# One core, a fused graph layer: offsets in slots of 16 words, norm statistics a tile ahead, one edge load and one one-hot per tile

## Chip, cores and metric

One Trainium2 chip, one core. The metric is the device time in microseconds (us) of one execution of the program. The kernel works in fp32; TensorE multiplies either fp32 or pairs of fp32r halves (a "hi" part and what is left of it, "lo").

## The reference

12,500 nodes with 128 features, 200,000 edges with 48 features, `dst` sorted. What is computed, cut to its core:

```python
h = jnp.maximum(_layernorm(x, axis=-1), 0.0)
agg_edge = jax.ops.segment_sum(edge_attr_48, dst, num_segments=12500)     # 12500 x 48
collected = jnp.concatenate([h, agg_edge], axis=1)                        # 12500 x 176
u = jax.nn.silu(collected @ W1 + b1)                                      # 256 wide
u = jax.nn.silu(u @ W2 + b2)                                              # 256 wide
out = x + h + (u @ W3 + b3)                                               # 12500 x 128
```

The only irregular part is the segment sum: the rows of `edge_attr` are added up by their destination.

## The kernel before

The nodes are cut into `NT` = 28 tiles of 448 nodes (the last one 404), the sorted edges into 391 groups of 512, 14 groups to a tile (`GPT`), seven to a half (`HALF`). A group lies on 128 partitions with four edges each. Its edges hit a window of at most 42 neighbouring nodes, so its sum is a matrix product: a one-hot matrix (edge against node of the window) made by VectorE's `onehot_of`, times the edges' features. `sum_tile` does this for 14 groups into the PSUM bank `stage`; ScalarE copies it to `staged` (`stage_sums`); `place_batch` then adds each group's 42 columns at the right place of the tile's bank `agg_ps`, by a matrix product with the identity whose output address is a register. Those registers are the group's **offsets**: 14 integers of `offset_row`, an SBUF tensor with one word per group, which `offsets_of` loads into registers of TensorE's sequencer. Batch `b` takes groups 14b-3 to 14b+10 (`EARLY` = 3); batch 0 takes 11 (words 0 to 10), the last one 16.

Every engine runs its own program; semaphores tie them together. The order of work is written out by hand in the `step` functions, one step per tile: steps 1 to 3 unrolled, 4 to 21 in a loop that does two steps a turn, 22 to 29 unrolled (`pipeline`). In step i

- TensorE does layer 1 of tile i-1, `offsets_of(i+1)`, `sum_tile(i+1)`, layer 3 of tile i-2, the transposes of tile i, `place_batch(i+1)`, layer 2 of tile i-1, in this order;
- VectorE does `relu_lo(i-1)`, `carry_over(i-1)`, the norm statistics of tile i (`load_stats`, bn_stats over x), `agg_lo(i-1)`, `aggregate_stats(i)`, the first one-hot half of tile i+2, `shift_of_norm(i)`, the lo parts of h1 and `add_x(i-1)`, the second one-hot half, `add_b3(i-1)`, and `finish(i-2)`, which makes the output tile;
- GpSimd does one power, (var+eps)^-0.5 (`rstd_of(i)`);
- ScalarE does the relu and hi parts, the SiLUs of layers 2 (tile i-2) and 1 (tile i-1), the normalised x (`normalize(i)`) and `stage_sums(i+1)`;
- SyncE issues all DMAs: first edge half of tile i+3, x of tile i+1, second edge half of tile i+3, store of tile i-2. Each waits in SyncE's queue until its buffer is free: the edge halves for `s_summed` (a half summed in step i), x for `s_plain` (`add_x(i-1)` is done, the last reader of that x buffer), the store for `s_out` (`finish(i-2)`).

Edges, one-hots and x are double buffered by the tile's parity.

Of the kernel before, what the change touches and what calls it, by code (L numbers as in the profile page):

```python
# [25 lines left out]
ALU = mybir.AluOpType  # L26
# [7 lines left out]
def gnn_kernel(nc, x, dst, edge_attr, W1, b1, W2, b2, W3, b3, out):  # L34
# [3 lines left out]
    P = 128  # L38
# [26 lines left out]
    assert N * GROUP == NPG * E and E % PER == 0 and N % PER == 0  # L65
    PAIRS = GPT // 2
# [16 lines left out]
    with ExitStack() as ctx:  # L83
        def sb(name, shape, dt=F32):
            return ctx.enter_context(nc.sbuf_tensor(name, shape, dt))
# [38 lines left out]
        offset_row = sb("offset_row", [1, ROWS * P], I32)  # L124
# [88 lines left out]
        s_edges = [sem(f"edges_loaded{k}") for k in range(4)]  # L213
# [71 lines left out]
        def _(sp):  # L285
# [5 lines left out]
            def load_edges(i, parity, half):  # L291
                n, full = groups_of(i, half)
                slot = 2 * parity + half

                wait(sp, s_summed, 2 * (i - 2) + half + 1)
                e0 = (i * GPT + half * HALF) * GROUP
                sp.dma_start(raw[:, slot, 0:full].rearrange("p g j d -> p g (j d)"),  # L297
                             edge_attr[bass.ds(e0, full * GROUP), :].rearrange(
                                 "(g p j) d -> p g (j d)", p=P, j=PER)).then_inc(s_edges[slot], 16)
                if full < n:  # L300
                    sp.dma_start(raw[0:TAIL_P, slot, full].rearrange("p j d -> p (j d)"),
                                 edge_attr[E - TAIL_P * PER:E, :].rearrange(
                                     "(p j) d -> p (j d)", j=PER)).then_inc(s_edges[slot], 16)
# [42 lines left out]
            for t in (2, 3):  # L346
                for half in range(2):
                    load_edges(t, t % 2, half)
# [16 lines left out]
            def step(i, parity):  # L365
                if has(i, -3, NT):
                    load_edges(i + 3, 1 - parity, 0)
                if has(i, -1, NT):
                    load_x(i + 1, 1 - parity)
                if has(i, -3, NT):  # L370
                    load_edges(i + 3, 1 - parity, 1)
                if has(i, 2, NT):
                    store(i - 2, parity)
# [8 lines left out]
        def _(pool):  # L382
# [23 lines left out]
            def step(i, parity):  # L406
                if has(i, 0, NT):
                    rstd_of(i, parity)
# [3 lines left out]
            pool.iota(tile_i[:, :], pattern=[[1, TILE]], base=0, channel_multiplier=0).then_inc(s_pool_zero, 1)  # L412
            pipeline(pool, step)
# [115 lines left out]
        def _(dve):  # L529
# [106 lines left out]
            def make_onehot(i, parity, half):  # L636

                wait(dve, s_summed, 2 * (i - 2) + half + 1)
                onehot_of(i, parity, half).then_inc(s_onehot, 1)

# [12 lines left out]
            dve.tensor_copy(offset_row[:, 0:P], z3[0:1, 0, :]).then_inc(s_off0, 1)  # L653
# [21 lines left out]
            dve.tensor_copy(offset_row[:, P:], z3[0:1, 1:ROWS, :].rearrange("p q d -> p (q d)"))  # L675
# [3 lines left out]
            for half in range(2):  # L679
                make_onehot(2, 0, half)  # L680

            def general_path():
# [31 lines left out]
                dve.wait_ge(s_onehot, 6)  # L714
# [93 lines left out]
            def step(i, parity):  # L808
                if has(i, 1, NT):
                    relu_lo(i - 1)  # L810
                    carry_over(i - 1, 1 - parity)
                if has(i, 0, NT):
                    load_stats(i, parity)
                    dve.wait_ge(s_stats, i + 1)
                if has(i, 1, NT):
                    agg_lo(i - 1)
                if has(i, 0, NT):
                    aggregate_stats(i, parity)
                if has(i, -2, NT):
                    make_onehot(i + 2, parity, 0)  # L820
                if has(i, 0, NT):
                    shift_of_norm(i, parity)
# [4 lines left out]
                if has(i, -2, NT):  # L827
                    make_onehot(i + 2, parity, 1)
# [8 lines left out]
        def _(pe):  # L837
# [63 lines left out]
            def sum_tile(i, parity):  # L901
# [160 lines left out]
```

## Time and profile before

| | |
|---|---|
| median of 3 runs | 417.44 us (416.64 to 420.57) |
| the profiled execution: its own time, and its span | 418.25 us, 416.5 us |
| busy share of the span: TensorE matmuls, weight loads | 80%, 72% |
| VectorE, ScalarE, GpSimd | 64%, 51%, 15% |
| mean granted TensorE clock | 0.967 of full speed |
| DMA | 53.07 MB, mean 127 GB/s |

The span runs from the first to the last instruction; the 1.75 us beside it are start and end of the execution. A row of a timeline says when a run of instructions of one line started, how long it took, and in brackets how long its engine had been idle before it and which event ended that idleness; "issue" means that the profile shows nothing that the engine waited for. Rows of the sequencers (PEldq: TensorE's, SPq: SyncE's) are register, branch and DMA instructions and are not counted as busy.

### The profile page before, as it was taken

How to read it: one execution, taken by the hardware profiler on the slowest of the kernel's cores; microseconds unless marked ns; L12 is line 12 of the kernel's file. 1: busy time of each engine (PE TensorE's matmuls, PEld its weight loads, DVE VectorE, ACT ScalarE, POOL GpSimd, SP SyncE). 2: the span in 40 equal slices, each digit the busy share in tenths (PEclk: the TensorE clock that was granted, in tenths of full speed). 3: DMA queues.
4: the chain of work that ended last, by engine and by line, in shares of the span. 5: the costliest groups of instructions: out<-in, count | busy, mean ns of one | idle time of the engine just before them, and what ended most of it. 6: DMA issues, size and time to landing. Idle time of an engine off the chain costs nothing.

```text
span 416.5 us, 13441 instructions
## 1 busy us (share of the span) xinstructions
PE 331.1 (80%) x5150; PEld 300.3 (72%) x5151; DVE 267.1 (64%) x634; ACT 213.9 (51%) x406; POOL 60.8 (15%) x44
## 2 busy tenths in 40 slices
PE   6556777977797779877897779777977798778885
PEld 6445777966687668866787669666966787677875
DVE  7954558566766686668656766667566765785443
ACT  7643446346644564455544653456346644465372
POOL 2101011012211222022202220122012110110000
PEclk9967969999999999999999999999999999999999
DMA  7970524633664256533663356435632675340101
GB/s 215 290 216 2 155 58 124 178 105 84 169 176 132 82 138 176 160 89 104 176 171 91 94 172 176 107 82 164 176 106 77 171 179 147 101 121 24 44 22 43
DMA packets 79194, 53.07 MB, mean 127 GB/s; under 512 B 2912, under 2 KB 78778, under 8 KB 79168
## 3 DMA queue, kind: packets, MB, share of 16 engines
q1 hardware_dynamic: 79168, 52.70, 46.1%
q8 instruction: 19, 0.31, 0.3%
q14 instruction: 7, 0.06, 0.0%
HBM read 46.29 MB, written 6.40 MB: 127 GB/s over the span
## 4 chain that ended last, share of the span: by engine, by line
PE 40%; issue 21%; DMA 20%; DVE 13%; ACT 3%; SPq 2%; DVEq 0%; POOL 0%; ACTq 0%; POOLq 0%
DMA x_t<-in_x_dram 20%; PE stage L919 16%; PE z L997 6%; DVE onehot L632 6%; PE agg_ps L936 4%; DVE stats L606 3%; PE z L982 3%; PE z L986 2%; PE z L983 2%; SPq L297 2%; DVE meanvar L612 2%; PE tp L949 1%; PE z L965 1%; PE z L970 1%; PE z L971 1%
## 5 line engine op out<-in xcount | busy, mean ns | idle before, releaser
L919 PE MATMUL stage<-onehot,raw 128*48 128x42 f32 x3128 | 81.8, 221 | 61.7 <-issue 60.8
L919 PEld LDWEIGHTS stage<-onehot,raw 128*48 128x48 f32 x3128 | 78.7, 132 | 71.4 <-issue 71.3
L403 POOL TENSOR_TENSOR rstd<-vareps,minus_half 112x4 f32<-112x4 f32 (+1 forms) x28 | 57.6, 2059 | 334.9 <-DVE vareps L616 334.9
L632 DVE TENSOR_TENSOR onehot<-window,rel 128x1176 f32<-128x1176 f32 (+1 forms) x56 | 76.9, 1375 | 2.7 <-ACT rel L433 1.3
L805 DVE TENSOR_TENSOR out_t<-z,resid 112x512 f32<-112x512 f32 (+1 forms) x28 | 19.4, 691 | 71.3 <-PE z L997 71.3
L997 PE MATMUL z<-w,h 128*112 128x128 f32 (+1 forms) x448 | 56.2, 278 | 0.9 <-ACT h L491 0.8
L997 PEld LDWEIGHTS z<-w,h 128*112 128x112 f32 (+1 forms) x448 | 50.8, 177 | 2.7 <-issue 1.4
L441 ACT ACTIVATE staged<-stage 112x294 f32<-112x294 f32 x28 | 11.6, 416 | 68.4 <-PE stage L919 68.4
L936 PE MATMUL agg_ps<-staged,ident 112*48 112x42 f32 x782 | 42.5, 219 | 5.1 <-issue 5.1
L470 ACT ACTIVATE xn<-x_t,nmr,rstd 112x128 f32<-112x128 f32 (+1 forms) x112 | 45.9, 480 | 0.1
L936 PEld LDWEIGHTS agg_ps<-staged,ident 112*48 112x48 f32 x782 | 39.2, 129 | 9.2 <-issue 5.7
L491 ACT ACTIVATE h<-z,b2c 128x448 f32<-128x448 f32 (+1 forms) x56 | 35.0, 626 | 17.2 <-PE z L986 17.2
L982 PE MATMUL z<-h_hi,w_hi 128*128 128x448 f32 (+1 forms) x112 | 43.8, 391 | 0.0
L499 ACT ACTIVATE h<-z,b1c 128x448 f32<-128x448 f32 (+1 forms) x56 | 35.0, 624 | 15.9 <-PE z L971 15.9
L478 ACT ACTIVATE hT_hi<-tp 128x448 fp32r<-128x448 f32 (+1 forms) x28 | 15.2, 542 | 51.3 <-PE tp L949 51.2
L983 PE MATMUL z<-h_hi,w_lo 128*128 128x448 f32 (+1 forms) x112 | 40.8, 365 | 0.0
L779 DVE TENSOR_TENSOR h_lo<-h,h_hi 128x448 fp32r<-128x448 f32 (+1 forms) x56 | 34.7, 620 | 5.1 <-ACT h_hi L503 5.0
L484 ACT ACTIVATE agg_hilo<-agg 48x448 fp32r<-48x448 f32 (+1 forms) x28 | 16.1, 577 | 40.5 <-DVE agg L755 40.5
L606 DVE BATCH_NORM_STATS2 stats<-x_t 112x6 f32<-112x128 f32 (+1 forms) x112 | 24.4, 279 | 16.9 <-DMA x_t<-in_x_dram 16.8
L503 ACT ACTIVATE h_hi<-h 128x448 fp32r<-128x448 f32 (+1 forms) x56 | 32.2, 575 | 1.8
L986 PE MATMUL z<-h_lo,w_hi 128*128 128x448 f32 (+1 forms) x112 | 31.9, 365 | 0.0
L772 DVE SCALAR_TENSOR_TENSOR hT_lo<-tp,hT_hi 128x448 fp32r<-128x448 f32 (+1 forms) x28 | 17.4, 623 | 12.5 <-ACT hT_hi L478 12.5
(108 smaller groups left out, 415.9 us busy)
## 6 DMA issues: line engine op xcount, KB each, us to landing
raw<-in_edge_attr_dram SPq DMA_DIRECT2D x55, 672.0 KB, 6.2
x_t<-in_x_dram SPq DMA_DIRECT2D x27, 224.0 KB, 5.3
out_dram<-out_t SPq DMA_DIRECT2D x27, 224.0 KB, 4.6
dst_rows<-in_dst_dram SPq DMA_DIRECT2D x1, 512.0 KB
raw<-in_edge_attr_dram SPq DMA_DIRECT2D x1, 480.0 KB, 5.8
dst_rows<-in_dst_dram SPq DMA_DIRECT2D x1, 256.0 KB, 2.7
out_t<-in_L_gnn_W_dram SPq DMA_DIRECT2D x1, 256.0 KB, 8.2
x_t<-in_x_dram SPq DMA_DIRECT2D x1, 192.0 KB
```

Of the source, the lines that this page charges most:

```text
L403: pool.tensor_tensor(rstd[0:np_, parity], vareps[0:np_, :], minus_half[0:np_, :], ALU.pow).then_inc(s_rstd, 1)
L470: ln = act.activation(xn[0:np_, parity, q, :], x_t[0:np_, parity, q, :], ACT.Identity, bias=nmr[0:np_, parity, q:q + 1], scale=rstd[0:np_, ...
L491: act.activation(h2[:, m, 0:n], z[:, m, 0:n], ACT.Silu, bias=b2c[:, m:m + 1]).then_inc(s_h2, 1)
L499: act.activation(h1[:, m, 0:n], z[:, m, 0:n], ACT.Silu, bias=b1c[:, m:m + 1]).then_inc(s_h1, 1)
L606: st = dve.bn_stats(stats[0:np_, q, :], x_t[0:np_, parity, q, :])
L632: return dve.tensor_tensor(onehot[:, slot, 0:n * PER, :], window[:, :].unsqueeze(1).broadcast_to([P, n * PER, WINDOW]), cols.unsqueeze(2). ...
L919: mm = pe.matmul(stage[at:at + ED, pair * WINDOW:(pair + 1) * WINDOW], raw[0:rows, 2 * parity + half, k, j, :], onehot[0:rows, 2 * parity ...
L936: mm = pe.matmul(banks[0:ED, bass.ds(offset, WINDOW)], ident[0:ROW2 + ED, at:at + ED], staged[:, parity if k >= 0 else 1 - parity, group / ...
L982: pe.matmul(z[:, m, 0:n], w2_hi[:, k, cols], h1_hi[:, k, 0:n], start=(k == 0), stop=False)
L983: pe.matmul(z[:, m, 0:n], w2_lo[:, k, cols], h1_hi[:, k, 0:n], start=False, stop=False)
L986: mm = pe.matmul(z[:, m, 0:n], w2_hi[:, k, cols], h1_lo[:, k, 0:n], start=False, stop=(k == M - 1))
L997: mm = pe.matmul(z3[0:np_, q, :], h2[:, k, q * np_:(q + 1) * np_], w3[:, k, :], start=(k == 0), stop=(k == M - 1))
```

## The change

- `offset_row` gets a slot of 16 words per batch (`SLOT`), with group k of batch b (k from -3) at word 16b+k+3. VectorE fills it with three strided copies in place of one, twice. `offsets_of(b)` reads from word 16b (batch 0 from word 3). The number of words that are loaded stays 11, 14 and 16.
- The statistics, the power and the shift of the norm run one tile ahead, for tile i+1 in step i; tile 1's are made before the first step.
- VectorE's order in a step is new: `add_x`, `carry_over`, `relu_lo`, `agg_lo`, one-hots of tile i+2, `load_stats(i+1)`, `add_b3`, `aggregate_stats(i+1)`, both lo parts, `shift_of_norm(i+1)`, `finish`.
- SyncE's order is x, edges, store. From tile 2 on the edges of a tile are one DMA (waiting until the whole of the tile before in that buffer is summed) and its one-hots one instruction; TensorE waits once for each per tile.

```diff
+    SLOT = 16
-        offset_row = sb("offset_row", [1, ROWS * P], I32)
+        offset_row = sb("offset_row", [1, NT * SLOT], I32)
...
+            def load_tile(i, parity):
+                full = sum(groups_of(i, half)[1] for half in range(2))
+                slots = raw[:, 2 * parity:2 * parity + 2].rearrange("p s g j d -> p (s g) (j d)")
+
+                wait(sp, s_summed, 2 * (i - 2) + 2)
+                sp.dma_start(slots[:, 0:full], edge_attr[bass.ds(i * GPT * GROUP, full * GROUP), :].rearrange(
+                    "(g p j) d -> p g (j d)", p=P, j=PER)).then_inc(s_edges[parity], 16)
...
             def step(i, parity):
-                if has(i, -3, NT):
-                    load_edges(i + 3, 1 - parity, 0)
                 if has(i, -1, NT):
                     load_x(i + 1, 1 - parity)
                 if has(i, -3, NT):
-                    load_edges(i + 3, 1 - parity, 1)
+                    load_tile(i + 3, 1 - parity)
                 if has(i, 2, NT):
                     store(i - 2, parity)
...
             def step(i, parity):
-                if has(i, 0, NT):
-                    rstd_of(i, parity)
+                if has(i, -1, NT):
+                    rstd_of(i + 1, 1 - parity)
...
+            def make_onehots(i, parity):
+
+                n = sum(groups_of(i, half)[0] for half in range(2))
+                wait(dve, s_summed, 2 * (i - 2) + 2)
+                cols = rel[:, :, :].rearrange("p g j -> p (g j)")[:, bass.ds(i * GPT * PER, n * PER)]
+                slots = onehot[:, 2 * parity:2 * parity + 2].rearrange("p s e w -> p (s e) w")
+                dve.tensor_tensor(slots[:, 0:n * PER, :],
+                                  window[:, :].unsqueeze(1).broadcast_to([P, n * PER, WINDOW]),
+                                  cols.unsqueeze(2).broadcast_to([P, n * PER, WINDOW]),
+                                  ALU.is_equal).then_inc(s_onehot, 1)
...
-            dve.tensor_copy(offset_row[:, 0:P], z3[0:1, 0, :]).then_inc(s_off0, 1)
+            offsets_into(0, EARLY, GPT)
+            offsets_into(1, 0, GPT, FULL0 - 1)
+            offsets_into(FULL0, 0, REST0).then_inc(s_off0, 1)
...
-            dve.tensor_copy(offset_row[:, P:], z3[0:1, 1:ROWS, :].rearrange("p q d -> p (q d)"))
+            offsets_into(FULL0, REST0, GPT)
+            offsets_into(FULL0 + 1, 0, GPT, NT - 2 - FULL0)
+            offsets_into(NT - 1, 0, NG + EARLY - (NT - 1) * GPT)
...
-            for half in range(2):
-                make_onehot(2, 0, half)
+            load_stats(1, 1)
+            dve.wait_ge(s_stats, 2)
+            aggregate_stats(1, 1)
+            make_onehots(2, 0)
+            shift_of_norm(1, 1)
...
             def step(i, parity):
                 if has(i, 1, NT):
+                    add_x(i - 1, 1 - parity)
+                    carry_over(i - 1, 1 - parity)
                     relu_lo(i - 1)
-                    carry_over(i - 1, 1 - parity)
-                if has(i, 0, NT):
-                    load_stats(i, parity)
-                    dve.wait_ge(s_stats, i + 1)
+                    agg_lo(i - 1)
+                if has(i, -2, NT):
+                    make_onehots(i + 2, parity)
+                if has(i, -1, NT):
+                    load_stats(i + 1, 1 - parity)
+                    dve.wait_ge(s_stats, i + 2)
                 if has(i, 1, NT):
-                    agg_lo(i - 1)
...
+                    add_b3(i - 1, 1 - parity)
+                if has(i, -1, NT):
+                    aggregate_stats(i + 1, 1 - parity)
                 if has(i, 1, NT):
                     h1_lo_part(i - 1, 0)
-                    add_x(i - 1, 1 - parity)
                     h1_lo_part(i - 1, 1)
...
-                if has(i, 1, NT):
-                    add_b3(i - 1, 1 - parity)
+                if has(i, -1, NT):
+                    shift_of_norm(i + 1, 1 - parity)
                 if has(i, 2, NT):
                     finish(i - 2, parity)
...
-                    offset_row[0:1, bass.ds(b * GPT + first, last - first)], engines=[mybir.EngineType.PE],
+                    offset_row[0:1, bass.ds(b * SLOT + (first + EARLY), last - first)], engines=[mybir.EngineType.PE],
...
                         if k % HALF == 0:
-                            pe.wait_ge(s_edges[slot], 16 * slot_turn(i, parity) + (16 if full < n else 0))
-                            pe.wait_ge(s_onehot, 2 * i + k // HALF + 1)
+                            if isinstance(i, int) and i < 2:
+                                pe.wait_ge(s_edges01[slot], 16)
+                                pe.wait_ge(s_onehot, 2 * i + k // HALF + 1)
+                            elif k == 0:
+                                pe.wait_ge(s_edges[parity], 16 * (slot_turn(i, parity) - 1) + (16 if total < GPT else 0))
+                                pe.wait_ge(s_onehot, i + 3)
```

## Rows read from the trace of the kernel before

**Rows 1.** Windows of two tile periods: us; PE, PEld, DVE, ACT, POOL busy; PEclk; DMA

```profile
181.61:195.20 13.59, 11.15 (x182) 10.14 (x183) 9.33 (x22) 7.08 (x15) 2.11 (x1) 1.00 0.50 135
195.20:208.75 13.55, 11.09 (x183) 10.14 (x183) 9.50 (x23) 7.08 (x16) 2.24 (x1) 1.00 0.46 135
```

**Rows 2.** Timeline, TensorE in the period from 181.61 (start, us, engine, line)

```profile
178.78 0.36 PE L971 MATMUL z<-agg_hilo,w1e_lo 112*128 112x448 f32 x1
...
181.61 2.72 PE L919 MATMUL stage<-onehot,raw 128*48 128x42 f32 x112 [2.46 <-issue]
...
190.54 0.37 PE L965 MATMUL z<-hT_hi,w1x_hi 128*128 128x448 f32 x1
...
195.20 2.72 PE L919 MATMUL stage<-onehot,raw 128*48 128x42 f32 x112 [2.44 <-issue]
...
199.69 0.55 PE L949 MATMUL tp<-ident,xn 112*128 112x112 f32 x4
```

**Rows 3.** The waits view, TensorE's sums (us in total, times, longest)

```profile
PE stage L919 <- issue: 60.8, 26, 2.6
```

**Rows 4.** Line L892, the offsets' register load, in five windows: ns min/median/max

```profile
L892 PEldq TENSOR_LOAD <-offset_row x18: 3332/3336/3344, 83.0 to 315.2; - x18
...
L892 PEldq TENSOR_LOAD <-offset_row x1: 1520/1520/1520, 27.3 to 27.3; - x1
...
L892 PEldq TENSOR_LOAD <-offset_row x1: 3343/3343/3343, 28.9 to 28.9; - x1
...
L892 PEldq TENSOR_LOAD <-offset_row x1: 3336/3336/3336, 178.0 to 178.0; - x1
...
L892 PEldq TENSOR_LOAD <-offset_row x1: 3800/3800/3800, 382.4 to 382.4; - x1
```

**Rows 5.** Line L270 on TensorE's sequencer: the load of one word

```profile
L270 PEldq TENSOR_LOAD <-any_invalid x1: 319/319/319, 32.3 to 32.3; - x1
```

**Rows 6.** Timeline, the early stretch around tiles 1 to 4

```profile
51.02 0.87 DVE L606 BATCH_NORM_STATS2 stats<-x_t 112x6 f32<-112x128 f32 x4 [3.74 <-DMA x_t<-in_x_dram]
...
52.60 0.47 PE L970 MATMUL z<-agg_hilo,w1e_hi 112*128 112x448 f32 x1 [2.12 <-DVE agg_hilo L765]
...
56.13 4.71 PE L919 MATMUL stage<-onehot,raw 128*48 128x42 f32 x112 [1.83 <-issue]
```

**Rows 7.** Timeline, VectorE, ScalarE and GpSimd from 184.82 to 197.49

```profile
186.30 0.69 DVE L805 TENSOR_TENSOR out_t<-z,resid 112x512 f32<-112x512 f32 x1 [2.29 <-PE z L997]
...
187.99 0.61 DVE L755 TENSOR_TENSOR agg<-agg_ps,agg_carry 48x448 f32<-48x448 f32 x1
...
189.16 0.87 DVE L606 BATCH_NORM_STATS2 stats<-x_t 112x6 f32<-112x128 f32 x4 [0.43 <-DMA x_t<-in_x_dram]
...
190.06 0.62 DVE L765 TENSOR_TENSOR agg_hilo<-agg,agg_hilo 48x448 fp32r<-48x448 f32 x1
...
190.71 0.38 DVE L612 BATCH_NORM_AGGREGATE meanvar<-stats 112x2 f32<-112x6 f32 x4
...
191.38 1.38 DVE L632 TENSOR_TENSOR onehot<-window,rel 128x1176 f32<-128x1176 f32 x1
191.52 2.11 POOL L403 TENSOR_TENSOR rstd<-vareps,minus_half 112x4 f32<-112x4 f32 x1 [11.28 <-DVE vareps L616]
...
194.06 1.63 ACT L470 ACTIVATE xn<-x_t,nmr,rstd 112x128 f32<-112x128 f32 x4
194.37 0.68 DVE L786 SCALAR_TENSOR_TENSOR resid<-xn,x_t 112x512 f32<-112x512 f32 x1
...
196.80 0.69 DVE L796 TENSOR_TENSOR resid<-resid,b3r 112x512 f32<-112x512 f32 x1
```

**Rows 8.** The DMA view from 182 to 196: issues, KB each, us to landing

```profile
raw<-in_edge_attr_dram SPq DMA_DIRECT2D x2, 672.0 KB, 6.0
x_t<-in_x_dram SPq DMA_DIRECT2D x1, 224.0 KB, 5.1
```

**Rows 9.** x loads (L310) over the whole run: min/median/max to landing

```profile
DMA to landing us min/median/max: 2.7/5.3/7.5
```

More of the change, by code:

```diff
@@ L212, in gnn_kernel @@
         s_carry0_act = sem("carry_zeroed_by_act")
-        s_edges = [sem(f"edges_loaded{k}") for k in range(4)]
+        s_edges01 = [sem(f"edges_of_0_and_1_loaded{k}") for k in range(4)]
+        s_edges = [sem(f"edges_loaded{k}") for k in range(2)]
         s_onehot = sem("onehot_ready")
@@ L291, in load_edges @@
             def load_edges(i, parity, half):
-                n, full = groups_of(i, half)
-                slot = 2 * parity + half
-                wait(sp, s_summed, 2 * (i - 2) + half + 1)
                 e0 = (i * GPT + half * HALF) * GROUP
[L297 to L303, printed above, removed]
+                sp.dma_start(raw[:, 2 * parity + half].rearrange("p g j d -> p g (j d)"),
+                             edge_attr[bass.ds(e0, HALF * GROUP), :].rearrange(
+                                 "(g p j) d -> p g (j d)", p=P, j=PER)).then_inc(s_edges01[2 * parity + half], 16)
+            def load_tile(i, parity):
[4 more added lines that the diff above has]
+                    "(g p j) d -> p g (j d)", p=P, j=PER)).then_inc(s_edges[parity], 16)
+                if full < GPT:
+                    sp.dma_start(slots[0:TAIL_P, full], edge_attr[E - TAIL_P * PER:E, :].rearrange(
+                        "(p j) d -> p (j d)", j=PER)).then_inc(s_edges[parity], 16)
             def load_x(t, parity):
@@ L346, in _ @@
             for t in (2, 3):
-                for half in range(2):
-                    load_edges(t, t % 2, half)
+                load_tile(t, t % 2)
             def general_loads():
@@ L412, in _ @@
             pool.iota(tile_i[:, :], pattern=[[1, TILE]], base=0, channel_multiplier=0).then_inc(s_pool_zero, 1)
+            rstd_of(1, 1)
             pipeline(pool, step)
@@ L636, in make_onehot @@
             def make_onehot(i, parity, half):
-                wait(dve, s_summed, 2 * (i - 2) + half + 1)
                 onehot_of(i, parity, half).then_inc(s_onehot, 1)
+            def make_onehots(i, parity):
[7 more added lines that the diff above has]
+                                  ALU.is_equal).then_inc(s_onehot, 1)
             def weights_lo():
@@ L652, in _, with offsets_into @@
             dve.wait_ge(s_small0T, 1)
-            dve.tensor_copy(offset_row[:, 0:P], z3[0:1, 0, :]).then_inc(s_off0, 1)
+            place_row = z3[0:1, :, :].rearrange("p q d -> p (q d)")
+            def offsets_into(b, first, last, many=1):
+                g0 = b * GPT - EARLY + first
+                into = offset_row[:, b * SLOT:(b + many) * SLOT].rearrange("p (b k) -> p b k", k=SLOT)[:, :, first:last]
+                return dve.tensor_copy(into, place_row[:, g0:g0 + many * (last - first)].rearrange(
+                    "p (b k) -> p b k", b=many))
+            FULL0 = (P + EARLY) // GPT
+            REST0 = (P + EARLY) % GPT
+            offsets_into(0, EARLY, GPT)
+            offsets_into(1, 0, GPT, FULL0 - 1)
+            offsets_into(FULL0, 0, REST0).then_inc(s_off0, 1)
             dve.wait_ge(s_rel, 1)
@@ L678, in _ @@
             dve.wait_ge(s_rel, ROWS)
-            for half in range(2):
-                make_onehot(2, 0, half)
+            load_stats(1, 1)
[3 more added lines that the diff above has]
+            shift_of_norm(1, 1)
             def general_path():
@@ L713, in general_path @@
                 turn(0, gen_rel, g["ok1"], ALU.add)
-                dve.wait_ge(s_onehot, 6)
+                dve.wait_ge(s_onehot, 5)
                 turn(1, rel, g["shift"], ALU.subtract)
```

8 lines of the change are left out of this document (removed).

## The prediction

> **What bounds the kernel now.** I read the windows of two whole tile periods first, from one `sum_tile` to the next [rows 1]. A period takes 13.57 us (the mean of 13.59 and 13.55); TensorE's matmuls fill 11.1 of it, VectorE 9.4, ScalarE 7.1, GpSimd 2.2, and the DMA engines are half busy at 135 GB/s. So no engine is full, but TensorE is nearest. The timeline then shows where the other 2.45 us are: in one place, ahead of `sum_tile` (L919), with "issue" as the releaser [rows 2]. The waits view adds this up to 60.8 us in 26 places [rows 3], by far TensorE's largest idle time. In the rest of the period its matmuls follow one another without a hole.
>
> "Issue" says that no other engine is late. The work there is that of TensorE's own sequencer: `offsets_of` (L892), which loads 14 words of `offset_row` into registers before the sums are issued. Its rows name the cost [rows 4]: the load at 178.0 takes 3.34 us and ends at 181.34, the sums begin at 181.61 [rows 2]. It starts 0.8 us before the last matmul of layer 1 starts (178.78), so that much of it is hidden, and it is the last to finish ahead of the sums. Whatever it gets shorter, the period gets shorter, until something else is late.
>
> Besides, there is an early stretch in which TensorE waits for another engine: at 52.60 it had stood 2.12 us for `agg_lo` (L765), because VectorE's statistics ahead of it in the queue had waited 3.74 us for x [rows 6]. The sum after that took 4.71 us where 2.72 are usual [rows 2, 6], the same instructions at a lower granted clock.
>
> **The load.** The change does not alter how many words are loaded, only where they begin. The rows give the price of a load by its length: 0.319 us for one word [rows 5], 3.34 for 14 and 3.80 for 16 [rows 4]. These three lie on one line, 0.087 + 0.232 per word. The 11 words of batch 0 would then take 2.64 us; they took 1.52 [rows 4]. What sets that load apart is its start: word 0 of the tensor, while batch b starts at word 14b-3, which is odd for every b. The 18 loads in the loop start at all odd places relative to 16 words and lie between 3.332 and 3.344 us, so crossing some boundary costs nothing; what counts is the start itself. Two words at a time from an even start would make six reads of 11 words, 0.087 + 6 x 0.232 = 1.48, close to 1.52. With the change every slot starts at a multiple of 16 words from the place where the load of 1.52 us started.
>
> So a load of 14 from a slot is 7 reads of (1.52 - 0.087)/6 = 0.239 us, 0.087 + 1.67 = 1.76 us. The bounds: four words at a time where they are whole (two fours and three singles make 1.52, so a four is 0.37) give 0.087 + 3 x 0.37 + 2 x 0.232 = 1.66, plain proportion, 14/11 of 1.52, gives 1.93, and a price that has nothing to do with the start leaves 3.34. I take 1.76, a saving of 1.58 us, because the one row of an even start is the nearest.
>
> The Trainium skill (Runtime: NRT & Kernel Launch, section Instruction fetch mechanics) says that such a load costs about 200 ns per register, even in bulk. By that an estimate of 14 x 0.2 = 2.8 us would hold before and after, and the change would take nothing here. The trace agrees for odd starts (0.232 us a word) and not for batch 0 (0.138); this is the third rival below.
>
> Is all of the saving on the path? In the period of rows 2 the load would end at 179.8, the sums could start at 180.03, and the last matmul of layer 1, which started at 178.78, leaves the array about 0.2 us later. The load is still what ends last, by 1 us, so all 1.58 us count. The count: batches 2 to 26 are 25 x 1.58 = 39.5; batch 27 has 16 words, 8 reads, 2.0 us against 3.80, so 1.8; batch 1, loaded before the first step with nothing beside it, 1.58; batch 0 now starts at word 3, odd, so 11 words cost 2.64 and 1.12 are lost. Together 41.8 us.
>
> **Statistics ahead, new order on VectorE.** In the steady period this takes nothing off TensorE's path, since `agg_lo` ended at 190.68 [rows 7] and layer 1 wants it 0.6 us after its start at 190.54 [rows 2]: just in time. It matters because this chain (x lands, statistics, `agg_lo`) would be late once the load is short. In the new order VectorE does after `finish` (186.30): 0.69, `add_x` 0.68, `carry_over` 0.61 and 0.2, `relu_lo` 0.62, `agg_lo` 0.62 [rows 7] (0.62 from the row of L765, for both), with 0.3 of handing over: ready at 190.0, 0.5 ahead of layer 1's start and over 1 ahead of where it is used. These times hang on TensorE's sums and matmuls, not on the load, so they keep their distance when the period shrinks. `relu_lo` now stands behind `carry_over`, which waits for `place_batch`; in the first step that makes layer 1 start some 0.3 us later and its `agg_lo` come 0.15 us sooner, nothing in sum. ScalarE is not on the path: xn is done at 195.69 [rows 7], TensorE transposes it at 199.69 [rows 2], and 2.4 us of these 4.0 are left.
>
> The early wait of 2.12 us goes, because x is then asked for right after `add_x`; the gap behind it was 1.83 instead of 2.46 [rows 2, 6], so at most 1.5 us net; I take 1.3. The slow clock behind it (2.0 us in that sum) came when TensorE had stood still twice in a few microseconds; I take 1.8 with what follows it, bounds 0 and 2.
>
> **One edge transfer, one one-hot, fewer waits.** One-hots: two of 1.38 us become one of about 2.7 [rows 7], used a step later, hidden. Edges: the first half leaves 1.4 us later, and is needed a whole period later still. The removed waits stand in a stream of matmuls without holes. The three offset copies run twice in place of one copy, some 0.3 us more before the first step, beside GpSimd's and ScalarE's work. Nothing for each, within 0.5 us.
>
> **The new ring.** The change closes a loop through VectorE's queue that was not there: `finish`, then `add_x`, which lets SyncE ask for x of the next tile, then its statistics, `add_b3`, `aggregate_stats`, GpSimd's power, the shift, and behind it the next `finish`. Its length: 0.69 + 0.68 + 0.1 to SyncE + L + 0.87 + 0.69 + 0.81 (from L612 to the power's start) + 2.11 + 0.2 = 6.15 + L, with L the time from x's issue to its landing [rows 7]. The ring holds the period above 12.0 if L is over 5.85. Before, L was 2.7 to 7.5 with a median of 5.3 [rows 9]; in the period shown it was 5.1, with one half of the edges (672 KB, 6.0 us) issued ahead of it and one behind [rows 8]. Now all 1344 KB are issued at the end of the sum, at 184.3, and x follows after `add_x`, near 187.8, 3.5 us later. I take L at 4 to 5.5: the DMA engines have worked off much of the edges by then. The ring is then 10.2 to 11.7 and does not bind; VectorE has the rest as slack.
>
> **Sum.** 418.25 - 41.8 (loads) - 1.3 (early wait) - 1.8 (clock) = 373.35 for an execution like the profiled one, which was 0.81 above the median; so **372.5 us**. The period should be near 12.0.
>
> **Rivals.**
> 1. *The ring binds a little.* L between 6.1 and 7 makes the period 12.25 to 13.15, 0.25 to 1.15 over 12.0 in 25 steps: 379 to 401. For it: six tenths of a period of DMA work stand ahead of x, and 7.5 has happened. Against: x is asked for 3.5 us after the edges. 14%.
> 2. *The ring binds above the old period, slower.* It decides from L = 7.4 (6.15 + 7.4 = 13.55). If x had to wait for the whole 1344 KB, L near 8.5 gives a period of 14.65, 1.1 more than before in 25 steps: 418 + 27 less the early gains, about 442. For it: the statistics now lie in front of `finish`; against: no x load of 27 took as long. 4%. The Trainium skill (DMA: Bandwidth & Descriptors, section Queues, rings and completion order) says that each DMA engine consumes one queue's descriptors in ring order, which is for rivals 1 and 2; no row here shows the order of single descriptors.
> 3. *The start of a load does not count*, and batch 0's was short for another reason (its place at the first use). Then only the early gains stay: 418.25 - 3.1 - 0.81 = 414.3. Against it: 1.12 us under the line that three other lengths share. 8%.
> 4. *The load is cheaper still*, wholly hidden: the period falls to TensorE's 11.1 or the ring's 11.4, 0.6 less in 25 steps, 357. 8%.
>
> **How the numbers follow.** The forecast has 66%, and its own range is 368 to 377 (loads at 1.66 to 1.93 us are 2.5 us below to 4.3 above; the early gains may be 3 less). To leave out no more than 2 in 10 the range takes in the lower half of rival 1 and part of rival 4: 363 to 388. A measurement of this kernel can tell about 1%, that is 4.2 us. Faster by more: forecast, rivals 1 and 4, 88%; within: rival 3, 8%; slower: rival 2, 4%.
>
> **What would show it.** In the profile after: L892 at about 1.76 us for 14 words, 2.0 for 16, 2.64 for the first; the idle time before L919 down from 2.46 to near 0.9; periods of 12.0; no wait of L970 for L765; x landing within 5.5 us and L606 waiting for it never long. If the periods are above 12.2 while the loads are short, the ring or VectorE is the reason, and `finish` (L805) will come later than TensorE's layer 3 (L997) allows. If L892 still shows 3.34, the step on the even start is wrong. The prediction would be wrong above all in that one step, since it rests on a single row.

## The result, and the profile after

The changed kernel took **359.63 us** (median of 4 runs, 359.18 to 359.88) against 418.63 us (4 runs, 416.64 to 420.57) of the kernel before: a ratio of 0.859, with an interval of 0.854 to 0.864. It is 14% faster, 12.9 us below the 372.5 that was forecast and below the range of 363 to 388. Its profiled execution took 359.18 us, with a span of 357.4.

The windows of the two tile periods that answer to [rows 1], with the same columns:

```profile
178.90:190.51 11.61, 11.15 (x183) 10.14 (x183) 8.67 (x18) 7.17 (x15) 1.27 (x1) 1.00 0.54 158
190.51:202.05 11.54, 11.09 (x183) 10.13 (x183) 9.34 (x22) 7.05 (x15) 1.41 (x1) 1.00 0.53 159
```

A period went from 13.57 to 11.58 us. The matmuls still fill 11.1 of it: 2.0 us of holes are gone and 0.46 are left. The timeline of TensorE around the sums, which are now L950, shows where these are, in the same place as before [rows 2]:

```profile
178.10 0.36 PE L1002 MATMUL z<-agg_hilo,w1e_lo 112*128 112x448 f32 x1
178.90 2.72 PE L950 MATMUL stage<-onehot,raw 128*48 128x42 f32 x112 [0.44 <-issue]
...
187.82 0.37 PE L996 MATMUL z<-hT_hi,w1x_hi 128*128 128x448 f32 x1
...
190.51 0.70 PE L950 MATMUL stage<-onehot,raw 128*48 128x42 f32 x22 [0.46 <-issue]
```

The waits view adds them up, against 60.8 us in 26 places before [rows 3]:

```profile
PE stage L950 <- issue: 9.5, 24, 0.5
```

And the register load itself, now L919: the whole run (ns, min/median/max), the window of batch 0, one in the loop, and that of the last batch with its 16 words [rows 4]:

```profile
L919 PEldq TENSOR_LOAD <-offset_row x28: 1112/1339/2823, 28.1 to 326.6; - x28
...
L919 PEldq TENSOR_LOAD <-offset_row x1: 2823/2823/2823, 28.1 to 28.1; - x1
...
L919 PEldq TENSOR_LOAD <-offset_row x1: 1337/1337/1337, 177.2 to 177.2; - x1
...
L919 PEldq TENSOR_LOAD <-offset_row x1: 1112/1112/1112, 326.6 to 326.6; - x1
```

Three numbers ask for an explanation. 14 words take 1.34 us and not the 1.76 of the forecast. 16 words take less than 14, which no price per word or per pair allows. And batch 0, now the one with an odd start, went from 1.52 to 2.82.

Two more rows tell what surrounds the load. The first is ScalarE's SiLU of the second half of layer 2 (L494), which TensorE's sequencer has to wait for before it issues the second half of layer 1. The other is a sum in the unrolled steps:

```profile
176.43 0.64 ACT L494 ACTIVATE h<-z,b2c 128x448 f32<-128x448 f32 x1 [0.61 <-PE z L1017]
...
282.87 2.72 PE L950 MATMUL stage<-onehot,raw 128*48 128x42 f32 x112 [0.19 <-issue]
```

The SiLU ends at 177.07 and the load starts at 177.2. In the kernel before it was 177.78 and 178.0. So the load starts right behind that wait, and what covers it are the five matmuls that are issued just before it, of which the first starts at 177.27 and the last at 178.10. The sum at 282.87 has a load of 1.35 us ahead of it like the others and yet a hole of only 0.19. The difference of some 0.26 us goes with register arithmetic that only the steps of the loop have: one instruction of 0.051 us ahead of the load at 177.2 and two of 0.076 and 0.032 behind it (L942, L943). What else is lost around them no row shows. The kernel before had this difference as well (holes of 2.35 to 2.46 us in the loop, 1.83 to 2.20 behind 14 words after it), and the change doesn't touch it.

VectorE, GpSimd and SyncE's DMA issues in the same period and at the start of the next, to be held against [rows 7]:

```profile
181.83 0.40 SPq L304 DMA_DIRECT2D raw<-in_edge_attr_dram  x1
...
183.59 0.69 DVE L835 TENSOR_TENSOR out_t<-z,resid 112x512 f32<-112x512 f32 x1 [1.79 <-PE z L1028]
184.31 0.69 DVE L816 SCALAR_TENSOR_TENSOR resid<-xn,x_t 112x512 f32<-112x512 f32 x1
...
185.34 0.32 SPq L315 DMA_DIRECT2D x_t<-in_x_dram  x1
...
190.11 0.87 DVE L609 BATCH_NORM_STATS2 stats<-x_t 112x6 f32<-112x128 f32 x4 [0.63 <-DMA x_t<-in_x_dram]
...
192.29 1.41 POOL L405 TENSOR_TENSOR rstd<-vareps,minus_half 112x4 f32<-112x4 f32 x1 [10.69 <-DVE vareps L619]
```

The ring that the prediction feared can be read off: x is asked for at 185.34, 3.5 us after the edges (181.83), and used at 190.11, 4.8 us later. `finish` (L835) still waits for TensorE, by 1.79 us. As long as it does, the ring has slack and doesn't bind.

### The profile page after: what moved, and what is told of

Its sections match the earlier page's. It is cut to its first block, busy times and chain, and to the rows that moved or that the text cites. A ratio compares the mean times of both kernels' runs of the same rounds, so it can differ in the third digit from the quotient of the medians.

```text
span 357.4 us, 13310 instructions
## 1 busy us (share of the span) xinstructions
PE 328.2 (92%) x5150; PEld 298.7 (84%) x5151; DVE 267.4 (75%) x612; ACT 214.3 (60%) x406; POOL 43.3 (12%) x44
## 4 chain that ended last, share of the span: by engine, by line
PE 88%; issue 5%; ACT 4%; DVE 2%; POOL 0%; ACTq 0%; POOLq 0%; DVEq 0%
PE stage L950 21%; PE z L1028 15%; PE agg_ps L967 11%; PE z L1013 8%; PE z L1017 6%; PE z L1014 6%; PE z L996 3%; PE tp L980 3%; PE z L1001 3%; PE z L1002 3%; PE z L997 3%; PE z L998 3%; ACT xn L473 1%; ACT agg_carry L430 1%; PE tp L883 1%
## 5 line engine op out<-in xcount | busy, mean ns | idle before, releaser
L950 PEld LDWEIGHTS stage<-onehot,raw 128*48 128x48 f32 x3128 | 74.4, 126 | 19.5 <-issue 11.9
L950 PE MATMUL stage<-onehot,raw 128*48 128x42 f32 x3128 | 77.5, 216 | 9.5 <-issue 9.5
L405 POOL TENSOR_TENSOR rstd<-vareps,minus_half 112x4 f32<-112x4 f32 (+1 forms) x28 | 40.1, 1434 | 284.9 <-DVE vareps L619 284.9
L649 DVE TENSOR_TENSOR onehot<-window,rel 128x2352 f32<-128x2352 f32 (+1 forms) x26 | 67.6, 2602 | 0.8
L494 ACT ACTIVATE h<-z,b2c 128x448 f32<-128x448 f32 (+1 forms) x56 | 35.4, 632 | 21.4 <-PE z L1017 20.3
L835 DVE TENSOR_TENSOR out_t<-z,resid 112x512 f32<-112x512 f32 (+1 forms) x28 | 19.4, 691 | 35.3 <-PE z L1028 35.3
L809 DVE TENSOR_TENSOR h_lo<-h,h_hi 128x448 fp32r<-128x448 f32 (+1 forms) x56 | 32.7, 621 | 6.9 <-ACT h_hi L506 6.9
L1013 PEld LDWEIGHTS z<-h_hi,w_hi 128*128 128x128 f32 x112 | 21.0, 187 | 2.6
L1017 PEld LDWEIGHTS z<-h_lo,w_hi 128*128 128x128 f32 x112 | 21.0, 188 | 1.9
(108 smaller groups left out, 414.0 us busy)
```

The source lines that it names most:

```text
L405: pool.tensor_tensor(rstd[0:np_, parity], vareps[0:np_, :], minus_half[0:np_, :], ALU.pow).then_inc(s_rstd, 1)
L494: act.activation(h2[:, m, 0:n], z[:, m, 0:n], ACT.Silu, bias=b2c[:, m:m + 1]).then_inc(s_h2, 1)
L649: dve.tensor_tensor(slots[:, 0:n * PER, :], window[:, :].unsqueeze(1).broadcast_to([P, n * PER, WINDOW]), cols.unsqueeze(2).broadcast_to([ ...
L809: dve.tensor_tensor(h1_lo[:, m, 0:n], h1[:, m, 0:n], h1_hi[:, m, 0:n].bitcast(F32), ALU.subtract).then_inc(s_h1_lo, 1)
L950: mm = pe.matmul(stage[at:at + ED, pair * WINDOW:(pair + 1) * WINDOW], raw[0:rows, 2 * parity + half, k, j, :], onehot[0:rows, 2 * parity ...
L1013: pe.matmul(z[:, m, 0:n], w2_hi[:, k, cols], h1_hi[:, k, 0:n], start=(k == 0), stop=False)
```

## The experiments

They come in three groups: which part of the change does it (first two), what the price of a load is (next three), and what is left behind it (the last five). Each ratio is to the kernel before as it ran beside the experiment, with a median of 419.3 to 421.2 us.

**Only the slots.** The kernel before, with nothing but the offsets moved:

```diff
-        offset_row = sb("offset_row", [1, ROWS * P], I32)
+        offset_row = sb("offset_row", [1, NT * SLOT], I32)
...
-                    offset_row[0:1, bass.ds(b * GPT + first, last - first)], engines=[mybir.EngineType.PE],
+                    offset_row[0:1, bass.ds(b * SLOT + (first + EARLY), last - first)], engines=[mybir.EngineType.PE],
```

> The kernel before with the slots of 16 words alone; order, statistics, halves of edges and one-hots as before. If the load is the whole of the gain, L892 is 1.34 us for 14 words as in the changed kernel, the period falls by 2.0 us to 11.6 and the time by 27 x 2.0 us to about 363. Rival: the chain x, statistics, agg_lo was only just in time before (0.5 us ahead of its use) and the statistics in front of agg_lo now stop layer 1: then L970 waits in most steps and the time stays at 375 to 395, and the other parts of the change earned the rest.

Measured: 361.90 us (361.15 to 362.42), ratio 0.862 (0.856 to 0.868). This part alone brings all but some 2 us of the change (the intervals of the two ratios overlap). The sums of the steady stretch follow each other as they do in the changed kernel, at 100.36, 111.90 and 123.48, a period of 11.56. What it lacks is early: here are TensorE's and VectorE's waits between 48 and 53 us, with the same pattern that [rows 6] showed in the kernel before.

```profile
48.92 0.87 DVE L607 BATCH_NORM_STATS2 stats<-x_t 112x6 f32<-112x128 f32 x4 [2.71 <-DMA x_t<-in_x_dram]
50.50 0.47 PE L985 MATMUL z<-agg_hilo,w1e_hi 112*128 112x448 f32 x1 [1.77 <-DVE agg_hilo L780]
52.11 4.21 PE L934 MATMUL stage<-onehot,raw 128*48 128x42 f32 x112
```

x late, the statistics late, `agg_hilo` late behind them, and then a sum of 4.21 us in place of 2.72.

**All but the slots.** The changed kernel with the two edits above undone and the old copies into `offset_row`.

> The changed kernel with the old places of the offsets (14b-3). If only the start of the load counts, the loads are 3.34 us again and the time is that of the kernel before less the early wait and clock, 412 to 417. Rival: the new order itself shortens the period (the waits that were taken out of the sums, or the fused instructions); then the period is clearly under 13.5 us and the time under 408.

Measured: 415.41 us (414.0 to 416.73), ratio 0.989 (0.982 to 0.997). The sums have the old hole again:

```profile
166.41 2.72 PE L936 MATMUL stage<-onehot,raw 128*48 128x42 f32 x112 [2.47 <-issue]
...
179.96 2.72 PE L936 MATMUL stage<-onehot,raw 128*48 128x42 f32 x112 [2.47 <-issue]
```

The wait for `agg_hilo` does not occur here, so the new order and the statistics ahead did remove it. But slow sums do occur:

```profile
54.91 3.71 PE L936 MATMUL stage<-onehot,raw 128*48 128x42 f32 x112 [2.18 <-issue]
...
69.71 4.22 PE L936 MATMUL stage<-onehot,raw 128*48 128x42 f32 x112 [2.20 <-issue]
```

Two more come at 234.36 (3.92) and 356.96 (4.04). The granted clock in the four is 0.68, 0.59, 0.65 and 0.62. In the changed kernel, which differs from this one only by the slots, all sums from tile 2 on take 2.69 to 2.72 us. So in the profiled executions the short load takes the slow clock away too, not only the hole. How many slow sums there are seems to differ from one execution of this kernel to the next: the mean granted clock of the four was 0.954 to 0.975 (at 416.7 and 414.0 us), and only one was profiled.

**Slots from word 2, and from word 4.** The changed kernel, with every slot 2 or 4 words further on:

```diff
+    SHIFT = 2
...
-                    offset_row[0:1, bass.ds(b * SLOT + (first + EARLY), last - first)], engines=[mybir.EngineType.PE],
+                    offset_row[0:1, bass.ds(b * SLOT + (first + EARLY + SHIFT), last - first)], engines=[mybir.EngineType.PE],
```

> The changed kernel with every slot two words further, so each load starts at 2 more than a multiple of 16. Pairs theory (two words at a time from an even start): the load stays near 1.76 us or less, time about 360 to 370. Fours theory (four words at a time, and only from a multiple of four words): no four is whole from the start, the load is 14 singles again, 3.34 us, and the time near 413. A theory in which the load goes on to the next multiple of four and takes fours from there: 2 + 12 words, 1.34 us, no change.

> The changed kernel with every slot four words further (16 bytes). Fours theory: 1.34 us a load as in the changed kernel, time 359 to 361. Rival, that the slot must start at a multiple of 8 or 16 words from the tensor's first word: the load is 3.34 us again (or 1.76 by pairs), the time 413 (or 370).

Measured: 415.55 us with 2 words, 359.27 with 4 (one run each). The loads of the first and then of the second:

```profile
L920 PEldq TENSOR_LOAD <-offset_row x28: 2820/3335/3802, 28.1 to 380.3; - x28
```

```profile
L920 PEldq TENSOR_LOAD <-offset_row x28: 1115/1335/2823, 28.4 to 326.7; - x28
```

A start at word 2 brings nothing: 14 words take 3.335 us, as from an odd one. That ends the reading of the prediction, two words at a time. A start at a multiple of four words (16 bytes), counted from the tensor's first word, is enough. From it 16 words take 1.11 us, which over the 0.087 of the prediction's line is 4 x 0.256. 14 words are three fours and two singles, 0.087 + 3 x 0.256 + 2 x 0.232 = 1.32, and 1.34 are measured.

**Whole slots.** If 16 words are cheaper than 14, every batch should load 16 and use the 11, 14 or 16 that it needs. The words between them are zeroed at the start (a third line, not shown):

```diff
-                    offset_row[0:1, bass.ds(b * SLOT + (first + EARLY), last - first)], engines=[mybir.EngineType.PE],
+                    offset_row[0:1, bass.ds(b * SLOT, SLOT)], engines=[mybir.EngineType.PE],
...
-                return offsets
+                return words[first + EARLY:last + EARLY]
```

> The changed kernel, but every batch loads its whole slot, 16 words from its first word (batch 0 too), and uses the 11, 14 or 16 that it needs; the unused words are zeroed at the start. Fours theory: four whole fours cost 0.087 + 4 x 0.256 = 1.11 us, less than 14 words (1.34), so the period falls by 0.23 us to 11.36, the first load from 2.82 to about 1.3, the time by 26 x 0.23 + 1.5 + 0.2 = 7.7 us to 352. If a load's first use carries 0.2 us of its own, the first of these equal loads is 1.3 and all others 1.11. Rival, cost per word whatever the grouping: 16 words cost more than 14 and the time rises by 2 us or more.

Measured: 350.81 us (350.21 to 351.35), ratio 0.836 (0.832 to 0.840).

```profile
L919 PEldq TENSOR_LOAD <-offset_row x28: 1102/1107/1292, 28.2 to 318.8; - x28
...
L919 PEldq TENSOR_LOAD <-offset_row x1: 1292/1292/1292, 28.2 to 28.2; - x1
```

The period is 11.35 and the hole before the sums 0.18 to 0.29 us in the loop, mostly 0.23; the unrolled steps show none. 28 equal loads also show something that the other kernels could not: the first takes 1.29 and the rest 1.10 to 1.11. The first load of a run costs 0.18 us more.

**Four loads of four words, between the matmuls of layer 1.** A load then stands behind the second and the fourth matmul of each half:

```diff
                     pe.matmul(z[:, m, 0:n], w1x_lo[:, cols], hT_hi[:, 0:n], start=False, stop=False)
+                    meanwhile()
                     pe.matmul(z[:, m, 0:n], w1x_hi[:, cols], hT_lo[:, 0:n], start=False, stop=False)
...
                     pe.matmul(z[:, m, 0:n], w1e_hi[:, cols], agg_hilo[:, 0:n], start=False, stop=False)
+                    meanwhile()
```

> As e5_load_16_words, but from step 1 on the slot is loaded as four loads of four words, set between the matmuls of layer 1 (after the 2nd, 4th, 7th and 9th of ten). If what counts is only that the sequencer is away from issuing while TensorE runs dry, four pauses of 0.34 us between matmuls of 0.2 us are mostly hidden by what is queued: the sums follow layer 1 with no gap, period 11.0 to 11.1, time 342 to 346. Rival: a load starts only when the matmuls ahead of it have left the queue; then the pauses add up in TensorE's stream, 4 x 0.3 us or so, and the time is 355 to 368. Second rival: with a period near 11.0 the ring through VectorE (finish, add_x, x load, statistics, power, shift) or VectorE itself binds at 11.2 to 11.5 and the time is 347 to 356.

Measured: 349.10 us (348.70 to 350.63), ratio 0.833 (0.828 to 0.837): some 1.7 us under whole slots and above the 342 to 346 that I had expected. It lies in the range of the second rival, but VectorE isn't what binds: `finish` waits for TensorE by 28.0 us in all (below). A load takes 0.33 us. The window from 100 to 200 us has no hole left on TensorE:

```profile
100.00:200.00 100.00, 100.00 (x1630) 89.57 (x1630) 81.80 (x180) 63.07 (x126) 11.96 (x9) 1.00 0.56 163
```

Yet the period is 11.2, and the timeline shows why: in the second half of layer 1 the matmuls start 0.23 and 0.24 us apart, where 0.20 to 0.21 is usual, and the sums 0.37 behind the last. No row has a hole, but the pauses show in the spacing.

```profile
181.84 0.36 PE L1010 MATMUL z<-hT_hi,w1x_lo 128*128 128x448 f32 x1
182.05 0.39 PE L1012 MATMUL z<-hT_lo,w1x_hi 128*128 128x448 f32 x1
182.28 0.36 PE L1015 MATMUL z<-agg_hilo,w1e_hi 112*128 112x448 f32 x1
182.52 0.44 PE L1017 MATMUL z<-agg_hilo,w1e_lo 112*128 112x448 f32 x1
182.89 0.91 PE L957 MATMUL stage<-onehot,raw 128*48 128x42 f32 x31
```

The loads alone don't do this. In the unrolled steps, with the same loads of 0.33 us, the matmuls start 0.19 to 0.22 us apart, the sums follow 0.28 to 0.30 behind the last, and four of the last five periods are 11.02 to 11.06 us. What the loop has besides is register arithmetic, 0.046 to 0.065 us ahead of each load.

**Two loads of eight words, and one of sixteen.** The same, with fewer and longer loads: `meanwhile()` only behind the second matmul of each half, then only behind that of the first half.

> As e6_four_loads_in_layer1 with two loads of eight words, each after the second matmul of a half of layer 1: 0.087 + 2 x 0.256 = 0.60 us each instead of four of 0.33, and two address computations fewer. Theory that a pause is hidden by what is queued: behind the second matmul of a half TensorE has 0.4 us of queued work or less, so 0.2 us show twice, but 0.14 us of register instructions go; period 11.1 to 11.4 where e6 has 11.2, time 347 to 354. Rival, that only the sum of sequencer time counts: 1.2 + less overhead is less than 4 x 0.33 + 4 x 0.07, then 346 to 348.

> As e9 with one load of all 16 words after the second matmul of layer 1 (1.11 us), in place of behind the tenth (e5_load_16_words). If the queue ahead of TensorE holds only a few matmuls, the pause is as long here as behind layer 1 and the time is that of e5, 351, within 2. Rival: the queue is deep or shallow differently at the two places; with more hidden the time is near 345, with less it is over 355 (layer 1 stands for 0.7 us or more).

Measured: 352.10 us (351.63 to 352.75) with two loads of 0.59 us, ratio 0.840; 362.72 (362.09 to 363.04) with one of 1.11, ratio 0.865. One load in the middle of layer 1 is 12 us worse than the same load at its end. I had expected 351 us; it is the rival ("with less it is over 355") that came. The timeline of the kernel with one:

```profile
106.61 0.37 PE L1010 MATMUL z<-hT_hi,w1x_lo 128*128 128x448 f32 x1
107.44 0.44 PE L1012 MATMUL z<-hT_lo,w1x_hi 128*128 128x448 f32 x1 [0.47 <-issue]
...
108.95 0.37 PE L1016 MATMUL z<-agg_hilo,w1e_lo 112*128 112x448 f32 x1
109.25 0.83 PE L957 MATMUL stage<-onehot,raw 128*48 128x42 f32 x28
```

The two starts around the load are 0.83 us apart; at the end of layer 1, in the kernel with whole slots, the last matmul and the sums are 0.59 apart (184.73 and 185.32). The 0.30 us before the sums are not a pause of a load: they stand in the unrolled steps of the kernel with four loads too. Why less is covered in mid-layer shows in what the load starts behind:

```profile
105.36 0.64 ACT L494 ACTIVATE h<-z,b2c 128x448 f32<-128x448 f32 x1
```

Layer 1 may start when ScalarE's first SiLU of layer 2 has ended, at 106.00. The load starts at 106.3 and takes 1.11 us, with only the two matmuls of 106.41 and 106.61 issued ahead of it, and these cover 0.4 us. Behind layer 1 it starts right after the second SiLU as well (ended 183.70, load 183.9), but there five matmuls stand ahead of it. In the unrolled steps of the kernel with one load it is the same: SiLU ended 305.06, load 305.2. This is read from the traces; no run changed that wait alone.

**Four loads, with the rest of the change undone.** The fastest kernel with the old order on SyncE and VectorE, statistics in their own step, halves of edges and two one-hots (only SyncE's order is shown):

```diff
             def step(i, parity):
+                if has(i, -3, NT):
+                    load_edges(i + 3, 1 - parity, 0)
                 if has(i, -1, NT):
                     load_x(i + 1, 1 - parity)
                 if has(i, -3, NT):
-                    load_tile(i + 3, 1 - parity)
+                    load_edges(i + 3, 1 - parity, 1)
```

> The kernel before with slots and the four loads in layer 1, but with its own order: statistics of the same tile, halves of edges and one-hots. If statistics a tile ahead and the new orders matter once the load is gone, this is slower than e6 by more than the 2.3 us that separated e1 from the changed kernel: agg_lo comes at 9.1 us after the start of the sums and is wanted at 9.5, so the steady period should still be the same; I expect e6 plus 2 to 4 us. Rival: VectorE's wait for the power (0.9 us) and its own 9.4 us do not fit 11.0, then e6 plus 8 or more.

Measured: 357.25 us (356.41 to 358.47), ratio 0.853 (0.848 to 0.857), 8.1 us over the same loads in the new order. I had expected 2 to 4; the rival said 8 or more. Periods vary from 11.1 to 12.5. The waits view of this kernel, and below it that of the one with the new order:

```profile
DVE nmr L625 <- POOL rstd L404: 25.7, 28, 1.1
...
DVE stats L607 <- DMA x_t<-in_x_dram: 20.8, 24, 2.5
...
DVE out_t L820 <- PE z L1030: 8.0, 12, 3.5
...
PE z L999 <- DVE agg_hilo L780: 3.5, 4, 1.1
```

```profile
DVE out_t L835 <- PE z L1046: 28.0, 23, 4.2
...
DVE stats L609 <- DMA x_t<-in_x_dram: 16.3, 22, 1.5
...
DVE nmr L627 <- POOL rstd L405: 11.4, 27, 0.9
```

Read `finish` (`out_t`) first: it waits for TensorE 28.0 us in all in the new order, 8.0 in the old. That idle time is VectorE's slack, and the old order has spent it: 14.3 us more on GpSimd's power, 4.5 more on x. Where none is left, TensorE waits for `agg_hilo`. The 3.5 us of that row are not all of it, since a load that stands behind a late wait is covered by nothing: in one period `agg_hilo` is done at 162.11, the load behind it starts at 162.3, and the matmuls around it start at 162.23 and 162.73, 0.3 us further apart than usual and with no idle row. So the second part of the change is worth 2 us while the load holds the period at 11.6 and 8 once it is 11.2. Which piece of that part does it, order, statistics or one-hots, was not tried.

**Edges ahead of x.** The changed kernel with two requests on SyncE swapped:

```diff
             def step(i, parity):
-                if has(i, -1, NT):
-                    load_x(i + 1, 1 - parity)
                 if has(i, -3, NT):
                     load_tile(i + 3, 1 - parity)
+                if has(i, -1, NT):
+                    load_x(i + 1, 1 - parity)
```

> The changed kernel with SyncE's order turned: edges of tile i+3 first, x of tile i+1 behind them, so x is asked for only after the sums of its step (2.9 us after their start) and not 3 us before the step's matmuls. Ring theory: VectorE then stands at load_stats until x lands, with both lo parts of h1 behind it, and layer 2 waits for these: sum start + 3.3 + 5 (x) + 0.9 + 0.7 + 0.6 + 1.2 = 11.7 where layer 2 wants them at 7.3, so about 4.4 us more per period and a time of 450 to 480, above the kernel before. Rival: x's place in SyncE's order has slack and nothing moves (359 to 362).

Measured: 596.94 us (one run), at a mean granted clock of 0.80. The time lies far above the 450 to 480 that I had said. The timeline of one period, and the landing of x in the whole run:

```profile
193.48 2.72 PE L950 MATMUL stage<-onehot,raw 128*48 128x42 f32 x112
...
196.41 0.39 SPq L304 DMA_DIRECT2D raw<-in_edge_attr_dram  x1
196.99 0.75 SPq L315 DMA_DIRECT2D x_t<-in_x_dram  x1
...
204.59 0.88 DVE L609 BATCH_NORM_STATS2 stats<-x_t 112x6 f32<-112x128 f32 x4 [11.14 <-DMA x_t<-in_x_dram]
...
207.37 1.28 PE L1017 MATMUL z<-h_lo,w_hi 128*128 128x448 f32 x2 [6.47 <-DVE h_lo L809]
...
216.24 1.02 PE L950 MATMUL stage<-onehot,raw 128*48 128x42 f32 x20
```

```profile
DMA to landing us min/median/max: 2.9/7.3/7.6
```

Follow the chain: the sum ends at 196.2 and only then lets SyncE ask for edges, and x behind them; x lands 7.6 us later; the statistics stand ahead of `h_lo` in VectorE's queue, so TensorE gets `h_lo` at 207.37; layers 2 and 1 then take 8.9 us to the next sum. Everything lies end to end, 22.8 us (the mean of the 25 periods is 20.9). I had x landing in 5 us and not in 7.6, and had left out the lower clock: from 207.37 to the next sum it is 0.50, and these 8.9 us, with a wait of 1.36 for ScalarE in them, would have been 4.3 by my count. The ring of the prediction is real; the order x, edges, store is what keeps it short, since x gets some 3.5 us of distance to the edges and lands in 4.7 (median).

## Why it came out faster than predicted

**What bounds the kernel: right.** The hole before `sum_tile` was the load, and each tenth that it lost came off the period: 2.00 us less load, 1.99 less period.

**The place counts, not the length: right in kind.** The slots alone give 361.9 us, and the third rival, for which the start does not matter, is excluded by them. The step that failed is "a load of 14 from a slot is 7 reads of (1.52 - 0.087)/6 = 0.239 us, 0.087 + 1.67 = 1.76 us": **the term of the load is mis-sized**. It is 1.34 us, a saving of 2.00 and not of 1.58, since the loads of 4, 8, 14 and 16 words show words being read four at a time from a multiple of four, not in pairs. Its one row, 1.52 us for the 11 words of batch 0, held an extra that belongs to the first load of a run, about 0.2 us. Without it 1.30 are left, and 0.087 + 2 x 0.256 + 3 x 0.232 is 1.30: two fours and three singles. With it, pairs fitted by accident. The lower bound of 1.66 had the right scheme, fours, but took the price of a four from the same row, 0.37 for 0.256. So a bound that should have caught the case shared its error. For 16 words it was 2.0 forecast and 1.11 measured; for batch 0, 2.64 and 2.82, again the extra.

**The account**, profiled execution against profiled execution, span 416.5 to 357.4, 59.1 us less:
- loads of batches 3 to 27, between the sum of tile 2 and that of tile 27: 24 x 2.00 + 2.69 = 50.7. The prediction had 24 x 1.58 + 1.8 = 39.7. These 11.0 are most of the miss.
- loads of batches 0 to 2: forecast 2.0 together. The sum of tile 2 starts 0.35 earlier (42.14 to 41.79), so before it little was on the path: 1.7 less.
- early wait and slow clock: forecast 1.3 + 1.8 = 3.1. Between the same two sums 344.24 us became 286.10, 58.1 less, and 7.4 of them are not loads: 4.3 more than forecast. Slow sums are 4.6 of the 7.4 (4.71, 4.12 and 3.92 for 2.72 each, at a granted clock of 0.50, 0.61 and 0.65), and TensorE's waits for `agg_hilo` were 2.8 in the whole run. I had counted the slow sum of [rows 6], and not those at 71.59 and 290.52. Nor does the reason that I gave for the slow clock, that TensorE had stood still twice, fit these two: ahead of each stood one hole only, the usual one of the long load (2.20 and 2.35 us).
- after the last sum 0.6, forecast nothing.

The differences, 11.0 - 1.7 + 4.3 + 0.6, are the 14.2 us between the forecast span saving of 44.9 and the 59.1 measured.

**Statistics ahead and the new order: right.** The early wait for `agg_hilo` is gone; in the steady period nothing changed (11.56 with the slots alone, 11.58 with all). That some 3 us come from here fits the 5.7 between the kernel before and all but the slots (interval 1 to 8), and the 2 to 3 between the slots alone and the whole change. The load and this part are not quite additive, as the old order becomes dear once the period is short.

**One edge transfer, one one-hot, fewer waits: right at nothing**, as far as the steady period tells; they were not run alone.

**The ring: right.** L was taken at 4 to 5.5; its median is 4.7. GpSimd's power was taken at 2.11 and takes 1.3 to 1.4, so the ring is about 6.15 - 0.75 + 4.7 = 10.1 and even at 11.2 does not bind. Rivals 1 and 2 did not happen. The kernel with edges ahead of x shows that a late x can hold up the period, though x is also asked for later there.

**Rival 4**, the load cheaper still, is the one that came, with 357 for 359.6. It was right on the size but not quite on the form: the load is not wholly hidden. A hole of 0.46 us is left in the loop, and the early stretch makes up for this.

The Trainium skill (Runtime: NRT & Kernel Launch, section Instruction fetch mechanics) gives a TENSOR_LOAD about 200 ns per register, even in bulk; its section Terms describes that instruction with loads from HBM, while the ones here read SBUF. The runs come near it for starts off a multiple of four words (0.232 us a word) and not for the others (0.069 us a word with 16 words); for these loads the measurement decides.

The fastest version here is the changed kernel with four loads of four words in layer 1, 349.1 us, 17% under the kernel before. Loading the whole slot at the end of layer 1 is within 2 us of it for an edit of three lines.

## What to carry to other kernels

A sequencer's register load appears as "issue" idle time ahead of what follows it: find its row, and put what it reads at multiples of 16 bytes in whole fours, even if that loads words that nobody needs. Then look at the last wait that its sequencer passes before the load: in these traces only the work issued between the two covered it. A row from the first use of something holds more than its price; two bounds drawn from one such row are one bound. Before calling a reordering worthless, look at the slack of the engine it relieves: it may pay only after the next gain.

## What the runs showed of the hardware

- TensorE's register load: 0.087 us + 0.232 per word when read singly; four words in 0.256 when the load starts at a multiple of 16 bytes from the tensor's first word. From such a start 4 words took 0.33, 8 words 0.59, 14 words 1.34, 16 words 1.11 us; from word 2 or an odd word 14 took 3.34.
- The load starts 0.1 to 0.3 us behind the end of the event that TensorE's sequencer waited for last (177.07 and 177.2 in the changed kernel, 177.78 and 178.0 before, 106.00 and 106.3 with one load in layer 1).
- The first load of a run takes 0.18 to 0.22 us more (1.29 for 1.11, 1.52 for 1.30).
- Slow sums of 3.7 to 4.7 us, from tile 2 on, came in the three kernels with loads of 3.34 us ahead of the sums (three or four in each profile) and once with the slots alone, right behind a wait of 1.77 us (4.21, granted clock 0.59). None came in the others, that with edges ahead of x left aside; the longest there was 3.07, in the kernel with one load in layer 1. The sum of tile 1, which starts some 2 us behind an idle stretch of 4.1 us, took 3.5 to 4.4 us in every kernel (3.85 in the changed one, granted clock 0.66). The granted clock as a whole was 0.97 in the changed kernel and 0.80 in the one with edges ahead of x, where TensorE stood still for a third of each period; there the period of the timeline above has 0.72.
- In the steady stretch GpSimd's power on 112x4 took 2.1 to 2.2 us in the old order and 1.3 to 1.4 in the new one, where no one-hot runs on VectorE beside it. With long loads and the new order it is 1.32 as well, so it is the order that counts. That the one-hot is the cause was only argued.
- x (224 KB) lands in 4.7 us (median) when asked for some 3.5 us behind 1344 KB of edges, with a store of 224 KB between the two, and in 7.3 when asked for 0.6 us behind them.
